# Parting the two turns of y and the two products of the logits in the expert stage

## The reference, cut to what matters

```
h = L0_tok(x)
h = h + L0_attn(layernorm(h))
h = h + L0_ffn(layernorm(h))

# L0_ffn, D = 64, H = 16, E = 32
logits = xf @ router_w.T + router_b
idx = argmax(logits, axis=-1)
hid = relu(einsum('nd,ndh->nh', xf, W1[idx]) + b1[idx])
out = relu(einsum('nh,nhd->nd', hid, W2[idx]) + b2[idx])
```

## Time and profile before

| | us |
|---|---|
| median of 3 runs | 640.06 (638.38 to 641.61) |
| the profiled execution's own time | 639.99 |
| its span, first to last instruction | 637.9 |
| TensorE busy (share of span) | 563.0 (88%) |
| VectorE busy | 518.4 (81%) |
| ScalarE busy | 396.2 (62%) |
| GpSimd busy | 326.1 (51%) |

### The profile page before, as it was taken

How to read it: one execution, slowest core, us unless ns; L and a number is a source line. 1 busy time by engine, 2 the same in 40 slices (tenths; PEclk the granted TensorE clock), 3 DMA queues, 4 the chain that set the end, 5 groups by cost and what they waited for, 6 DMA issues and landing times. The chain is left out here.

```text
span 637.9 us, 18276 instructions
## 1 busy us (share of the span) xinstructions
PE 563.0 (88%) x7079; PEld 386.0 (61%) x7080; DVE 518.4 (81%) x940; ACT 396.2 (62%) x659; POOL 326.1 (51%) x355
## 2 busy tenths in 40 slices
PE   3696999999999999999866667659999999999995
PEld 3432888888888888888522223335555555555552
DVE  3988589999988999999499999958787777777762
ACT  3775477777777777777878666325555555455543
POOL 6503346655567766664499689553333333333320
PEclk9999599999999999999986988869999999999998
DMA  9602222224322222220000000000010101010101
GB/s 192 96 16 43 48 56 50 57 54 68 70 57 56 55 55 53 51 57 18 2 0 1 1 1 0 4 1 19 19 26 19 26 17 25 20 24 21 24 21 25
DMA packets 62376, 23.01 MB, mean 36 GB/s; under 512 B 45778, under 2 KB 62290, under 8 KB 62290
## 3 DMA queue, kind: packets, MB, share of 16 engines
q1 hardware_dynamic: 61472, 21.69, 16.7%
q10 hardware_dynamic: 690, 0.13, 0.1%
q0 software_dynamic: 128, 0.00, 0.0%
HBM read 5.02 MB, written 4.19 MB: 14 GB/s over the span
## 5 line engine op out<-in xcount | busy, mean ns | idle before, releaser
L624 ACT ACTIVATE work<-work 128x1024 f32<-128x1024 f32 x64 | 67.7, 1058 | 55.9 <-DVE work L682 55.8
L677 DVE TENSOR_REDUCE work<-psum 128x16 f32<-128x1024 f32 x64 | 78.0, 1219 | 23.2 <-PE psum L524 23.2
L539 PE MATMUL psum<-kc,work 128*128 128x128 f32 x512 | 76.0, 282 | 10.3 <-DVE work L694 7.1
L682 DVE TENSOR_TENSOR work<-psum,work 128x1024 f32<-128x1024 f32 x64 | 78.4, 1224 | 2.2
L1728 ACT ACTIVATE hid<-psum,b1c 128x512 f32<-128x512 f32 x96 | 58.9, 685 | 32.4 <-PE psum L1635 32.4
L489 POOL TENSOR_TENSOR work<-work 128x4 f32<-128x4 f32 x32 | 32.2, 1008 | 88.1 <-DVE work L719 88.1
L632 ACT ACTIVATE work<-psum 128x512 f32<-128x512 f32 x128 | 71.2, 591 | 9.1 <-PE psum L539 7.6
L1643 PE MATMUL psum<-x_t,w1x 64*64 64x256 f32 x1024 | 70.9, 393 | 0.0
L1618 POOL TENSOR_TENSOR m_sq<-m_xc 128x256 f32<-128x256 f32 x32 | 19.6, 612 | 99.5 <-DVE m_xc L1779 99.4
L539 PEld LDWEIGHTS psum<-kc,work 128*128 128x128 f32 x512 | 58.9, 144 | 18.8 <-DVE work L694 14.7
L555 PEld LDWEIGHTS psum<-work 128*64 128x64 f32 x2048 | 63.9, 141 | 6.3 <-ACT work L632 6.3
(11 more groups left out here) (192 smaller groups left out, 1239.6 us busy)
## 6 DMA issues: line engine op xcount, KB each, us to landing
work<-big_bc SPq DMA_DIRECT2D x256, 32.0 KB, 2.0
h_all<-in_x SPq DMA_DIRECT2D x16, 256.0 KB, 5.2
work<-big_a SPq DMA_DIRECT2D x32, 128.0 KB, 2.2
out<-out_st SPq DMA_DIRECT2D x128, 32.0 KB
w1x<-in_L_ffn_W SPq DMA_DIRECT2D x2, 128.0 KB, 4.3
kc<-constants SPq DMA_DIRECT2D x1, 202.0 KB, 2.9
w2x<-in_L_ffn_W SPq DMA_DIRECT2D x1, 128.0 KB, 3.7
work<-in_L_tok_qkv_w ACTq DMA_DIRECT2D x2, 32.0 KB, 3.6
```

The lines of the kernel that those rows point to most:

```text
L539: m = pe.transpose(banks[4 + half][:, n * P:n * P + P], prob[:, f, at:at + 2, :], ident)
L624: act.activation(prob[:, f], prob[:, f], ACT.Exp).then_inc(prob_done, 1)
L677: dve.tensor_reduce(top[:, f, :].rearrange("p (g h) -> p g h", g=4), sc, AX.X, ALU.max).then_inc(top_done, 1)
L682: dve.tensor_tensor(prob[:, f].rearrange("p (g h) k -> p g h k", g=4), sc, top[:, f, :].rearrange("p (g h) -> p g h", g=4).unsqueeze(3).br ...
```

## The change

The two turns of y (item 1) get parted: the first stays, two of the four parts of item 2 follow, then the second turn with y_turned, then the other two parts. Where item 2 isn't live (steps 0 and 1), the second turn follows the first at once. The wait for x_copied stands between the first turn and the first part, as it did between the pair and the parts. The two products of the logits (item 8) get parted by the two of b2: product 0, then the wait for o_copied and the b2 products, then product 1 with logits_done, then the second layer. Numbers of instructions, tiles, banks and waits stay as they are. The diff, whole but for its header:

```diff
@@ -1646,6 +1646,13 @@
                                   skip_group_check=True)
                     m.then_inc(x_half, 1)
 
+            def y_turn(n):
+                return pe.transpose(psum[:, 0, n * P:n * P + P], y_st[:, n, :], ident)
+
+            def logits(i, k):
+                return pe.matmul(psum[:, 1, 256 + k * 2 * NE:256 + k * 2 * NE + 2 * NE], x_t[:, (i - 1) % 2, k, :],
+                                 rwx[:, :, :], start=True, stop=True, skip_group_check=True)
+
             def body(i):
                 if live(i, 0):
                     pe.wait_ge(y_staged, i + 1)
@@ -1653,12 +1660,16 @@
                         pe.wait_ge(h_done, i)
                     if not first(i, 3):
                         pe.wait_ge(out_made, i - 3)
-                    for n in range(2):
-                        m = pe.transpose(psum[:, 0, n * P:n * P + P], y_st[:, n, :], ident)
-                    m.then_inc(y_turned, 1)
+                    y_turn(0)
+                    if not live(i, 2):
+                        y_turn(1).then_inc(y_turned, 1)
                 if live(i, 2):
                     pe.wait_ge(x_copied, i - 1)
-                    for g, b in X_PARTS[:4]:
+                    for g, b in X_PARTS[:2]:
+                        x_part(i - 2, g, b, True)
+                    if live(i, 0):
+                        y_turn(1).then_inc(y_turned, 1)
+                    for g, b in X_PARTS[2:4]:
                         x_part(i - 2, g, b, True)
                     if first(i, 2):
                         pe.wait_ge(masks_set, 1)
@@ -1697,16 +1708,16 @@
                         mask(g)
                 if live(i, 1):
                     pe.wait_ge(x_copied, i)
-                    for k in range(2):
-                        m = pe.matmul(psum[:, 1, 256 + k * 2 * NE:256 + k * 2 * NE + 2 * NE], x_t[:, (i - 1) % 2, k, :],
-                                      rwx[:, :, :], start=True, stop=True, skip_group_check=True)
-                    m.then_inc(logits_done, 1)
+                    logits(i, 0)
                 if live(i, 2):
                     if not first(i, 2):
                         pe.wait_ge(o_copied, i - 2)
                     for b in range(2):
                         pe.matmul(psum[64 * b:64 * b + 64, 6, 0:256], b2p[:, :], mark_t[:, b, :],
                                   start=True, stop=False, skip_group_check=True)
+                if live(i, 1):
+                    logits(i, 1).then_inc(logits_done, 1)
+                if live(i, 2):
                     for g in OUT_ORDER:
                         if g == 2:
                             pe.wait_ge(relu_dve, i - 1)
```

## The result

The changed kernel takes 657.19 us in the median of 4 runs (656.98 to 658.21), against 640.4 us before: ratio 1.0269, interval 1.024 to 1.0298. That is slower by some 17 us; 657.7 was forecast. The profiled execution took 656.98, with a span of 654.9.

A forecast was written before the change was run, and what follows sets the result against it. TensorE was taken to bound the expert stage, so added entries lengthen each step: 9.0 us for the y turns plus 8.7 for the logits, 17.7 on 639.99, gave 657.7 us (chance 0.80), range 647 to 663.

The forecast's parts named there:

- TensorE alone bounds the stage: Expert stage: one period's chain is TensorE's ten blocks, 6.40 us, so whatever lengthens its list lengthens every step.
- 0.15 an entry: On TensorE, each start of a block on another kind of tile costs 0.15 us, with or without a semaphore wait.
- The y turns, 9.0 us: Parting the y turns adds two entries, 0.30 us a step, over steps 2 to 31: 30 x 0.30 = 9.0 us.
- The edge: Step 2, mostly at 1.2 GHz: two entries at double price, 0.6, minus a covered wait of 0.31, again cost 0.30.
- The logits, 8.7 us: Parting the logits by b2 adds 0.28 us a step, over steps 2 to 32: 31 x 0.28 = 8.7 us.
- the sum by ends, 0.27: Logits, b2 and second layer, block lengths added from the chain: 2.57 us before, 2.84 after, so +0.27 a step.
- The moved signals cost nothing: Later y_turned and logits_done fit in the slack of their takers; 0.26 us stays in hand before the hid relu.
- The signs: Period 6.99 us, four more issue idles a step; turn 1 within 0.22 or second layer under 0.9 would be wrong.
- Rival A: Entries into turn 1 and logits 1 are free, their loads going ahead without a wait: 648 us, chance 0.10.
- B: Faster: loads of logits 1 and a turn hide under products of another tile, added entries free: 635 us, chance 0.03.
- C: Added running empty lowers TensorE's clock to 1.2 GHz for a tenth of the stage: 668 us, chance 0.05.
- D: Entries are paid, but something else sets the step's end, so no difference: 640 us, chance 0.02.

The follow-up runs named there:

- the halves: The change with only the y turns parted (650.22 us, ratio 1.0152) and with only the logits parted (648.35 us, 1.012), ratios to the kernel before.
- the run with the y turns beside the logits: Kernel before, with the next step's y turns put behind the logits on the same 128x128 tiles, one entry fewer a step: 635.49 us, ratio 0.9927.
- xh: The changed kernel with the two xh turns parted too, by two parts of the first layer's second half: 668.2 us, ratio 1.0419 to before.
- the interleaved turns: Kernel before, with the two o and two xh turns alternating, all on 128x128 tiles: 640.88 us, ratio 1.0011.
- the logits parted on 128x64: Kernel before, with each logits product cut in two for 128x64 tiles and the logits parted by b2 as in the change: 640.39 us, ratio 0.9993.

## Why the prediction was right, step by step

- **TensorE alone bounds the stage.** Right but for 0.02 us: 0.577 added to its list a step are 0.577 in the period, the halves add up, and what is taken from it in the run with the y turns beside the logits comes off as well. The chain named TensorE only, and yet ScalarE's first relu held the second layer for 0.023 a step.
- **0.15 an entry.** Right in size. By the periods it is 0.309 / 2 = 0.155 for the y border and 0.311 / 2 = 0.156 for xh. The logits' 0.266 lacks the 0.023 of the relu, which went as the second layer came later: (0.266 + 0.023) / 2 = 0.145. The entry taken away gave 0.167 with the same 0.023 in it: 0.144. That the price belongs to the kind of tile and not to the semaphore or the operands, which was argued from two rows, is now shown by the interleaved turns, by turn 1 without a wait, and by the logits parted on 128x64.
- **The y turns, 9.0 us.** 30 x 0.309 = 9.3; measured alone 1.52%, 9.7 us (8.5 to 11.1). The edge was wrong: in step 2 the parted turns were to cost 0.30, and from turn 0 to the first mark turn it is 2.88 us for 2.86 (424.59 to 427.47, before 424.69 to 427.55). The wait of 0.31 for VectorE's mark is gone there, and the added entries cost no more than about that.
- **The logits, 8.7 us.** 31 x 0.266 = 8.2; measured alone 1.2%, 7.7 us (6.1 to 9.3). The 0.28 was a trifle high. The sum has eight groups at 0.215 and 0.03 for the second layer's 1.75; the runs show what most of that 0.03 was, the relu's hold, which the change takes away, so the sum by ends, 0.27, was the better one.
- **The moved signals cost nothing.** Right: VectorE's stand before the relu is 0.21, for 0.26 forecast, and no wait of TensorE came up.
- **The signs.** The period is 6.991, for 6.99; turn 1 starts 0.33 behind the last group; the second layer starts 0.36 + 0.23 + 0.36 = 0.95 behind the first logit, over the 0.9. The four more "issue" idles are not in the list, as said above, which leaves the short ones out: that sign was badly chosen.
- **Rival A**, loads going ahead across the border: refuted by the 0.33 from the last group to turn 1 and the 0.23 from b2 to logits 1. On this point the rule of the Trainium skill in TensorEngine Tiling (Array Packing), Key Properties, that a change of tiling mode drains the engine, agrees with the 0.09 to 0.11 by which the added borders start late. **B**, faster through hidden loads: refuted, every added entry cost 0.14 or more; a load hides so only where the kind stays (b2 to logits 0.11). **C**, the clock: it stayed at 1.00 in the stage; of the page's digits after the 28th slice only the last is below 9, an 8 as before. **D**, no difference: the 17 us are there.
- What the prediction did not see: that the second layer stood at the edge of ScalarE's relu. It cost the forecast little, because the change moved the second layer later. For a change in the other direction it would have been the wrong step.

## What to carry to other kernels

Where TensorE bounds a stage, count the changes of the kind of tile in its order, price one from two blocks of the same form that differ only in what stands before them, and put blocks of one kind together; a block of another kind between two products, meant to cover their loads, adds two borders. A product may also be cut so that it takes its neighbour's tile. Before counting on such a saving, look for an engine that ends just as TensorE comes to need it: such a wait has no row as long as the weight-load port is still busy with the block before.

## What the runs showed of the hardware

- Behind a change of kind the next block starts 0.09 to 0.11 us late and its first load shows by 0.05; the size was the same for 64x64 to 128x128, 128x64 to 128x128 and 128x128 to 64x64, with a semaphore or without. Together 0.144 to 0.156 us by the periods, at the full clock.
- Not every change of rows or columns is one. From 128x128 to the 96-row, 64-column products of b2 there is a border (0.21 behind a logits instruction of 0.11); from their 96 rows to 128 rows at 64 columns there is none (0.13 from b2 to the second layer's start), nor from the mark turns' 96 columns to the o turns' 128, which take 0.25 and not 0.37.
- One 64x64 part alone takes as long as two on the four tiles: 0.58 and 0.59.
